# Four residual layers on one core: expert blocks beside the gates of the other half, two context chains, top-2 by VectorE's max search

## The chip, the cores and the metric

The kernel runs on one core of a Trainium2 chip. The metric is device time in microseconds (us) of one execution; less is better. The core's engines are PE (TensorE: matmuls and transposes), DVE (VectorE), ACT (ScalarE), POOL (GpSimd) and SP (here only a queue that issues DMAs; it is written SPq in the views). Each engine takes its instructions strictly in the order in which the program gives them; they meet through semaphores.

## The reference

x has 32 batches of 128 tokens of 128 values. Eight residual steps follow each other, each scaled by the tanh of a gate g. Cut to what matters:

```python
x = x + tanh(g0) * attention(heads=16, q=x_normed, kv=context)                    # "A0"
x = x + tanh(f0) * ffn(layernorm(x))                                              # "F0", hidden 512
x = x + tanh(g1) * attention(heads=16, over context and self)(layernorm(x))       # "A1"
x = x + tanh(f1) * block1(layernorm(x))     # "F1": causal attention, then 8 experts, top 2:
    t = rmsnorm(u, g2); probs = softmax(t @ router_w); vals, idx = top_k(probs, 2)
    w = vals / sum(vals); y = sum_k w_k * w2[e_k] @ (silu(w1[e_k] @ t) * (w3[e_k] @ t))    # hidden 256
x = x + tanh(g2) * attention(heads=8, kv=context)(layernorm(x))                   # "A2"
x = x + tanh(f2) * block2(layernorm(x))     # "E2": layernorm again, 8 experts, top 2, hidden 512, gelu
    tp, ti = top_k(softmax(xf @ Wg.T + bg), 2); tp = tp / (sum(tp) + 1e-8)
x = x + tanh(g3) * depool(layernorm(x), ctx)       # "context" work: norm of ctx, scan, picked rows
x = x + tanh(f3) * bitlinear_ffn(layernorm(x))     # quantized, hidden 512
```

## The kernel before

A planner written in Python (`make_plan`) decides the order of all work before the kernel is built. Each `do(kind, ...)` appends one step; each engine's program then walks through the list of steps and issues its part of each. So the order of the `do` calls is the order on every engine's queue and on SP's DMA queue. `reckon` gives the planner a cost in ns for each step by engine, and the planner keeps a clock for each engine from them. Work that is not part of the main loop is put on a list `side` with `soon` or `chain` (a chain is a list of units; each goes on the list when the one before it has been issued and its tokens are due). `run_side` takes the first unit of the list, by rank (0 first) and then age, for which `can` says yes: its needs are due by the planner's clock, and the engine that it begins on is at most 3000 ns ahead of PE by that clock. `drain(done)` issues side units until `done()` holds. `now()` gives the last tokens of every engine, which a step can wait for before it reuses memory.

The main loops are the attentions (A0, A1, the causal one of F1, and A2), batch by batch, with 16 preparations of pairs of batches (norm, transpose, `split` into three bf16 parts, store to DRAM, load back) as side chains. The maxima of each batch (`max_rows`) go through three small DMAs.

The expert layers work on groups g of four batches ("fronts", `sorted_front`), 8 of them, 4 in each half h. A front of E2 is: `n0` and `n1` layernorm of X into U, `n2` the second norm into a front buffer, `n3` `gate_turn` (four transposes), `n4` `gate_logits`, `n5` `gate_exp`, `n6` `gate_rank`, `n7` `gate_pick`, `n8` `place` (a prefix sum on PE that gives each token its row in its expert's region), `n9` four times `scatter` (2 indirect DMAs by POOL each, so 8 in a front), and `x_base`. A front of F1's experts ("E1") has one norm less. Fronts of even and of odd g are two lines; g can be ranked only when g-1 is placed. When the four fronts of a half are scattered, the half is sorted, and its 24 expert blocks of 256 rows can run (`blocks`: `block_table`, then for each block load, turn, weights, up, down, store). Then `fetch` (2 indirect DMAs by POOL for a batch) and `combine` bring the results back to X.

The stages around the change, in the order of the plan:

- F1's attention, with the fronts of E1 beside it; when half 0 is sorted, its blocks run beside the rest of the attention. Then `drain(lambda: not side)`: all fronts and all blocks of half 0 are finished. `after_f1 = now()` stands behind that drain.
- half 1's blocks of E1 beside the first 9 steps of A2 (at step 9 the plan drains until they are stored), then `moe2_load`, then the rest of A2 with fetches and combines of E1, with fronts of E2 as side work.
- `drain(lambda: not side)` again: all fronts of E2 are finished. Then one chain with half 0's blocks of E2, `half(0)` (fetches, and the last two layers' own work `own(g)` for g 0 to 3, in 2 lanes), half 1's blocks, `half(1)` (g 4 to 7, in 4 lanes). Beside it one chain of `setup` and the eight contexts `context(g)`: `cx_load`, `ends`, `end_marks`, a norm, `picks`, `up_scale`, `depool`, `pick_rows`. `own(g)` can pass `x4` (`x3_add`) only when the context of g is there.

On SP's queue `q_load` (the last layer's weights) waits for its need and holds everything behind it; DVE waits in its own `q_load` too.

Of the kernel before, what the change touches and what calls it, by code (L numbers as in the profile page):

```python
# [9 lines left out]
I32 = mybir.dt.int32  # L10
F32R = mybir.dt.float32r
# [85 lines left out]
def reckon(s):  # L97
# [218 lines left out]
class Memory:  # L316
    def __init__(self, nc, ctx, io):
# [58 lines left out]
        self.LG = sb("LG", [128, 2, 4, 8])  # L376
        self.GT = sb("GT", [128, 2, 4, 8])
# [60 lines left out]
        self.GM, self.DD = CF[:, 3840:4352], CF[:, 5376:5888]  # L438
        self.UP, self.CX = VSF[:, 0:512], VAF[:, 0:1024].rearrange("p (b d) -> p b d", b=4)
# [11 lines left out]
        self.EB = self.r32[:, :, :].rearrange("p a b -> p (a b)").bitcast(BF16)[:, 0:512].rearrange("p (k t) -> p k t", k=4)  # L451
# [45 lines left out]
def make_plan():  # L497
# [706 lines left out]
    E1 = experts_of(0, gi=5, chunks=2, xf=(("HB", 6), ("HB", 7)), t=(0, 1), big="big_at0", weight="router_w", scale="g2", bcol=None, plus=None)  # L1204
    E2 = experts_of(1, gi=6, chunks=4, xf=(("AT", 0), ("sp32", 0)), t=(2, 3), big="big_at", weight="WgT", scale="gamma", bcol="beta", plus=1e-8)

    def sorted_front(E, g):
        got, b0, k, h = {}, 4 * g, g % 2, g // 4

        def n0():  # L1210
            got["s"] = norm_in(("X", b0), 4, xs(b0, 4), twice="second")

        def n1():
            if E.i:
                got["u"] = norm_out(got["s"], ("U", b0), None, done="u")
                for j in range(4):
                    u_done[b0 + j] = got["u"]
            else:
                got["s"] = norm_in(("U", b0), 4, us(b0, 4), rms=True)

        def n2():
            got["n"] = norm_out(got["s"], E.xf[k], (E.xf_free[k], E.begin), second=(("U", b0), got["u"]) if E.i else None)
# [49 lines left out]
        return [*([n0] if E.i else []), n1, n2, n3, n4, n5, n6, n7, n8, *[(lambda j=j: n9(j), lambda: got["p"]) for j in range(4)], (base, ())]  # L1272

    def blocks(E, h, t_w, start, bank):
# [5 lines left out]
        def table():  # L1280
# [1701 lines left out]
```

## Time and profile before

| | |
|---|---|
| time, median of 3 runs (lowest to highest) | 2334.78 us (2333.24 to 2337.86) |
| the profiled execution, own time | 2332.09 us |
| its span, first to last instruction | 2330.3 us |
| busy: PE, PE weight loads | 1703.6 us (73%), 1207.5 us (52%) |
| busy: DVE, ACT, POOL | 1318.2 us (57%), 1025.1 us (44%), 684.4 us (29%) |
| mean granted TensorE clock | 0.832 of full speed |

The views used below: a table of stretches gives busy time of each engine in each stretch of the span, with granted clock (PEclk) and DMA share. A timeline gives instructions in order of time, merged when the same one follows itself (x4), with the idle time before them and what released them in brackets. Groups by line give count, busy us, mean ns of one, and idle time before. Times of a timeline are us from the start of the span.

### The profile page before, as it was taken

Reading aid. Unit: us, or ns where it says so; the run is one execution under the profiler, and the core shown is the slowest. Engines: PE = TensorE matmul, PEld = TensorE weight load, DVE = VectorE, ACT = ScalarE, POOL = GpSimd, SP = SyncE. Lnnn points to the kernel's source line nnn. Section 1 sums busy time; section 2 is a strip of 40 time slices with the busy share of each in tenths; the row PEclk is TensorE's granted clock in tenths of the full one; section 3 lists DMA queues with packets and bytes.
Section 4 is the critical chain, followed back from the end, with each engine's and each line's share of the span. In section 5 each row is a group of like instructions: output and inputs, shape, how many; then the busy total and the mean of one; then the engine's idle time right before and its main releaser. Section 6 shows DMA issues by size and latency. Waiting matters only on the chain. (4 is left out here: it accounts for less than half of the span.)

```text
span 2330.3 us, 42245 instructions
## 1 busy us (share of the span) xinstructions
PE 1703.6 (73%) x14898; PEld 1207.5 (52%) x14902; DVE 1318.2 (57%) x3879; ACT 1025.1 (44%) x2073; POOL 684.4 (29%) x1123
## 2 busy tenths in 40 slices
PE   2758879999679888899879974675473298687144
PEld 1435547677467666655545663554242187566032
DVE  4656664533456676557766543553577722365475
ACT  2435543433256565544434443442242065477165
POOL 4322100100422222134442124323535600612430
PEclk9978889999878888889988997886576599799566
DMA  6545546300155455312222122444360222212100
GB/s 176 125 85 113 124 145 201 73 1 0 25 101 96 90 111 97 92 45 54 52 54 59 43 64 59 102 121 144 84 138 28 66 62 71 77 51 64 36 19 19
DMA packets 189757, 184.47 MB, mean 79 GB/s; under 512 B 29508, under 2 KB 177924, under 8 KB 183556
## 3 DMA queue, kind: packets, MB, share of 16 engines
q1 hardware_dynamic: 180540, 145.04, 26.9%
q10 hardware_dynamic: 816, 19.92, 2.9%
q0 software_dynamic: 8192, 16.79, 2.5%
q8 instruction: 122, 2.00, 0.4%
q14 instruction: 87, 0.71, 0.1%
HBM read 119.47 MB, written 80.74 MB: 86 GB/s over the span
## 5 line engine op out<-in xcount | busy, mean ns | idle before, releaser
L2100 DVE TENSOR_REDUCE mneg<-psb 128x4 f32<-128x512 f32 (+1 forms) x576 | 386.1, 684 | 245.2 <-PE psb L1711 197.5
L2505 ACT ACTIVATE HB<-psb 128x512 f32<-128x512 f32 x384 | 222.8, 597 | 208.5 <-PE psb L1711 194.1
L1711 PE MATMUL psb<-K,Q 96*128 96x128 bf16 x1280 | 188.1, 249 | 68.1 <-DVE mneg L2100 37.7
L2738 POOL TENSOR_SCALAR rs<-mv 128x2 f32<-128x2 f32 (+1 forms) x96 | 22.7, 237 | 702.0 <-DVE mv L2060 693.0
L2505 ACT ACTIVATE HB<-psb,bias 128x512 f32<-128x512 f32 x192 | 132.0, 687 | 209.5 <-PE psb L1711 170.0
L1711 PE MATMUL psb<-Q,K 99*128 99x128 bf16 x1280 | 144.6, 244 | 92.2 <-DMA Q<-mT 91.0
L1711 PEld LDWEIGHTS psb<-K,Q 96*128 96x128 bf16 x1280 | 112.0, 111 | 125.5 <-DVE mneg L2100 50.8
L1711 PEld LDWEIGHTS psb<-Q,K 99*128 99x128 bf16 x1280 | 106.8, 111 | 125.4 <-issue 110.5
L1711 PE MATMUL psb<-K 128*128 128x256 f32 x576 | 152.4, 412 | 2.9 <-issue 2.1
L1711 PE MATMUL psb<-KS,Q 96*128 96x128 bf16 x1024 | 150.6, 238 | 4.8 <-DVE mneg L2100 4.3
L1711 PE MATMUL psb<-HB,VA 128*9 128x128 f32 (+1 forms) x2560 | 147.8, 307 | 8.1 <-ACT OE L2510 4.5
L1711 PEld LDWEIGHTS psb<-K 128*128 128x128 f32 x576 | 113.2, 207 | 18.9 <-issue 3.9
L1711 PE MATMUL psb<-HB,VS 128*9 128x128 f32 (+1 forms) x2048 | 109.7, 289 | 11.6 <-ACT OE L2510 7.5
L1711 PE MATMUL psb<-Q,KS 99*128 99x128 bf16 x1024 | 108.5, 233 | 2.2 <-DMA Q<-mT 2.2
L1711 PE MATMUL psb<-cnegb,identb 128*128 128x512 bf16 x256 | 107.4, 420 | 0.5 <-issue 0.5
L2318 DVE TENSOR_TENSOR K<-psb,HB 128x256 f32<-128x256 f32 x48 | 20.4, 424 | 153.2 <-PE psb L1711 114.1
L1723 PE MATMUL psb<-cst,OE 128*128 128x128 f32 x480 | 95.4, 324 | 14.6 <-ACT OE L2510 11.0
L1711 PEld LDWEIGHTS psb<-KS,Q 96*128 96x128 bf16 x1024 | 91.4, 106 | 25.8 <-issue 11.2
L1711 PEld LDWEIGHTS psb<-WB,HB 128*128 128x128 f32 x768 | 96.2, 197 | 14.8 <-issue 12.2
L1711 PE MATMUL psb<-WB,HB 128*128 x768 | 96.4, 280 | 9.9 <-ACT HB L2590 9.9
L1711 PE MATMUL psb<-biasT,selbb 96*128 96x512 bf16 x192 | 91.1, 474 | 1.8 <-issue 1.8
L1711 PEld LDWEIGHTS psb<-Q,KS 99*128 99x128 bf16 x1024 | 79.5, 105 | 22.2 <-issue 10.6
(464 smaller groups left out, 3984.0 us busy)
## 6 DMA issues: line engine op xcount, KB each, us to landing
tok_rows<-in_zero ACTq DMA_DIRECT2D x16, 1152.0 KB, 31.6
K<-sc_k SPq DMA_DIRECT2D x32, 384.0 KB, 5.2
Q<-sc_q SPq DMA_DIRECT2D x32, 384.0 KB
sc_q<-comp SPq DMA_DIRECT2D x48, 192.0 KB
K<-tok_rows SPq DMA_DIRECT2D x72, 128.0 KB
y_rows<-K SPq DMA_DIRECT2D x72, 128.0 KB
sc_q<-comp SPq DMA_DIRECT2D x48, 128.0 KB
vraw<-in_ctx SPq DMA_DIRECT2D x48, 128.0 KB, 6.8
```

Of the source, the lines that this page charges most:

```text
L1711: return pe.e.matmul(out, w, x, start=start, stop=stop, skip_group_check=True)
L1723: t = pe.e.transpose(o[:, 128 * j:128 * j + 128], src[:, 128 * j:128 * j + 128], ident)
L2100: t = e.tensor_reduce(m.mneg[:, s.b % 4, s.i * A.per:(s.i + 1) * A.per], PSB[s.use.bank].rearrange("p (h k) -> p h k", h=A.per), AX.X, ALU ...
L2318: v.done(e.tensor_tensor(y2, o2, m.b2bc[:, bass.ds(at_, 128)].unsqueeze(1).broadcast_to([128, 2, 128]), ALU.add), s.use.drained)
L2505: a.done(act(m.HB[:, s.slot, :], PSB[s.use.bank], ACT.Exp, bias=bz), s.use.drained)
L2738: then(e.tensor_scalar(r0, var, EPS, None, ALU.add))
```

## The change

Eight edits, in the planner unless said otherwise:

1. `after_f1` is taken right after the last step of F1's attention, and the drain behind it ends when half 0's blocks of E1 are done and half 1 is sorted, instead of when nothing is left. Half 1's blocks start as soon as half 1 is sorted and the attention is planned (`second1`). The two halves' block loads and stores get separate semaphores.
2. The drain behind A2 is gone. The blocks of E2 begin when half 0 is sorted (`table` returns False until then, and is tried again later).
3. The last layer's `setup` and the contexts begin when E2's half 1 is sorted (`third`), and the contexts run as two chains (even and odd g) with two sets of buffers (GM, DD, UP, CX, EB).
4. `gate_logits` finds the 8 values in order with `e.max` and their places with `e.max_index`, 4 of each; `gate_rank` and its 256-wide comparisons are gone; the softmax's sum is no longer needed but for E2's 1e-8.
5. `gate_pick` computes the two weights from two exponentials and the masks from the found indices.
6. `norm_out` of all fronts (two in E2, one in E1) goes from DVE to ACT. For E2's first norm POOL then adds a product and a negation (`shift`).
7. `x_base` stands ahead of the four scatters instead of behind them.
8. Ranks: E1's fetches 2 instead of 1; half 1's fetches of E2 2 instead of 1. Planner costs of the gate steps: see the diff.

```diff
-        "gate_logits": lambda: (("pe", 300), ("dve", 650)),
+        "gate_logits": lambda: (("pe", 1900), ("dve", 2200)),
         "gate_exp": lambda: (("act", 250),),
-        "gate_rank": lambda: (("dve", 2600),),
-        "gate_pick": lambda: (("dve", 2800),),
+        "gate_pick": lambda: (("dve", 1600),),
...
+        self.GM, self.DD = [CF[:, 3840:4352], CF[:, 4864:5376]], [CF[:, 5376:5888], CF[:, 4352:4864]]
+        self.UP = [VSF[:, 0:512], VSF[:, 512:1024]]
+        self.CX = [a.rearrange("p (b d) -> p b d", b=4) for a in (VAF[:, 0:1024], self.xn[:, :, :].rearrange("p a b -> p (a b)"))]
...
-            got["s"] = norm_in(("X", b0), 4, xs(b0, 4), twice="second")
+            got["s"] = norm_in(("X", b0), 4, xs(b0, 4), twice="second", by="act")
...
-                got["u"] = norm_out(got["s"], ("U", b0), None, done="u")
+                got["u"] = norm_out(got["s"], ("U", b0), None, done="u", by="act")
...
+            got["n"] = norm_out(got["s"], E.xf[k], (E.xf_free[k], E.begin), second=(("U", b0), got["u"]) if E.i else None, by="act")
...
-            do("gate_rank", g=g, big=E.big, need=got["t"], free=E.begin, done=inc("dve", "ranked"))
-
-        def n7():
             got["k"] = inc("dve", "picked")
-            do("gate_pick", g=g, i=E.i, big=E.big, plus=E.plus, gi=E.gi, need=t_tg, done=got["k"])
+            do("gate_pick", g=g, i=E.i, plus=E.plus, gi=E.gi, need=(got["t"], t_tg), done=got["k"])
...
-        return [*([n0] if E.i else []), n1, n2, n3, n4, n5, n6, n7, n8, *[(lambda j=j: n9(j), lambda: got["p"]) for j in range(4)], (base, ())]
+        return [*([n0] if E.i else []), n1, n2, n3, n4, n5, n6, n8, (base, ()), *[(lambda j=j: n9(j), lambda: got["p"]) for j in range(4)]]
...
+            if E.sorted[h] is None:
+                return False
...
+    after = {}
+
+    def second1():
+
+        if "f1" not in after:
+            return False
+        chain(blocks(E1, 1, t_m, after["f1"], misc), 3)
+        return None
+
     def end1(h):
-        if h == 0:
-            chain(blocks(E1, 0, t_m, E1.begin, misc), 3)
+        chain([second1] if h else blocks(E1, 0, t_m, E1.begin, misc), 3)
...
     run_f1()
-    drain(lambda: not side)
-    after_f1 = now()
+    after_f1 = after["f1"] = now()
+    drain(lambda: E1.done[0] and E1.sorted[1])
...
-    E2.begin, E2.end = after_f1, lambda h: None
+    E2.begin, E2.end = after_f1, lambda h: third() if h else None
...
-    chain(blocks(E1, 1, t_m, after_f1, misc), 3)
     begin2()
-    chain([(lambda b=b: fetch1(b), lambda b=b: E1.stored[b // 16] or ()) for b in range(B)], 1)
+    chain([(lambda b=b: fetch1(b), lambda b=b: E1.stored[b // 16] or ()) for b in range(B)], 2)
...
     run2(more)
-    drain(lambda: not side)
...
+    def third():
+
+        L3["units"] = setup, context, *_ = layer3((now(), E2.xf_free))
+
+        def contexts():
+            for c in range(2):
+                chain([f for g in range(c, NG, 2) for f in context(g)], 1)
+
+        chain([*setup, contexts], 1)
...
     def half(h):
+        if "units" not in L3:
+            return False
...
-        chain([(lambda b=b: fetch2(b), ()) for b in range(16 * h, 16 * h + 16)], 1)
+        chain([(lambda b=b: fetch2(b), ()) for b in range(16 * h, 16 * h + 16)], 1 + h)
...
-    chain([*setup, *[f for g in range(NG) for f in context(g)]], 1)
...
-        v.wait_ge(v.step(e.tensor_reduce(s0, L, AX.X, ALU.max)))
-        v.done(e.tensor_tensor(L, L, wide(s0), ALU.subtract), s.done)
-
-    def gate_rank(s):
-        _, L, T, s0, s1 = gate_views(s.g)
-        big0, big1 = big(s.big)
-        v.wait_ge(s.need, s.free)
-        v.wait_ge(v.step(e.tensor_reduce(s0, L, AX.X, ALU.add)))
+        for j in range(4):
+            t = e.max(V[:, j, :], L[:, j, :])
+        v.wait_ge(v.step(t))
+        v.done(e.tensor_tensor(E, m.LG[:, s.g % 2], V[:, :, 0:1].broadcast_to([128, 4, 16]), ALU.subtract), s.done)
+        for j in range(4):
+            t = e.max_index(ix[:, j, :], V[:, j, :], L[:, j, :])
+        v.step(t)
+
+    def gate_pick(s):
+        bs = slice(4 * s.g, 4 * s.g + 4)
+        E, ix, s0, s1 = m.EG[:, s.g % 2], m.ix[:, s.g % 2], m.small[:, 0, bs], m.small[:, 1, bs]
+        M, ek = m.pick, m.ek[:, s.i, :, bs]
+        v.wait_ge((v.chain, v.n), s.need)
+        t = v.step(e.tensor_copy(ek.rearrange("p k b -> p b k"), ix[:, :, 0:2]))
+        t2 = v.step(e.tensor_tensor(s0, E[:, :, 8], E[:, :, 9], ALU.add))
+        v.wait_ge(t)
+        number = C("blocks")[:, 0:8].unsqueeze(1).unsqueeze(1).broadcast_to([128, 2, 4, 8])
+        v.wait_ge(v.step(e.tensor_tensor(M[:, :, :, :], number, ek.unsqueeze(3).broadcast_to([128, 2, 4, 8]), ALU.is_equal)))
+        v.done(e.tensor_tensor(m.pickb[:, :, :], M[:, 0], M[:, 1], ALU.add), s.done)
+        if s.plus:
+            v.wait_ge(v.step(e.tensor_reduce(s1, E[:, :, 0:8], AX.X, ALU.add)))
+            v.wait_ge(v.step(e.scalar_tensor_tensor(out=s0, in0=s1, scalar=s.plus, in1=s0, op0=ALU.mult, op1=ALU.add)))
         v.wait_ge(v.step(e.reciprocal(s1, s0)))
-        v.wait_ge(v.step(e.tensor_tensor(L, L, wide(s1), ALU.mult)))
-        pj = L.unsqueeze(2).broadcast_to([128, 4, 8, 8])
-        pi = L.unsqueeze(3).broadcast_to([128, 4, 8, 8])
-        low = C("low").rearrange("p (i j) -> p i j", i=8).unsqueeze(1).broadcast_to([128, 4, 8, 8])
-        e.tensor_tensor(big0, pj, pi, ALU.is_gt)
-        v.wait_ge(v.step(e.tensor_tensor(big1, pj, pi, ALU.is_equal)))
-        v.wait_ge(v.step(e.tensor_tensor(big1, big1, low, ALU.mult)))
-        v.done(e.tensor_tensor(big0, big0, big1, ALU.add), s.done)
-        v.wait_ge(s.done)
-
-    def gate_pick(s):
-        bs, L, T, s0, s1 = gate_views(s.g)
-        big0, _ = big(s.big)
-        M = m.pick
-        v.wait_ge(v.step(e.tensor_reduce(T, big0, AX.X, ALU.add)))
-        e.tensor_scalar(M[:, 0], T, 0.5, None, ALU.is_lt)
-        e.tensor_scalar(M[:, 1], T, 1.0, None, ALU.is_equal)
-        e.tensor_scalar(m.pickb[:, :, :], T, 1.5, None, ALU.is_lt)
-        v.wait_ge(v.step(e.scalar_tensor_tensor(out=T, in0=T, scalar=1.5, in1=L, op0=ALU.is_lt, op1=ALU.mult)))
-        v.wait_ge(v.step(e.tensor_reduce(s0, T, AX.X, ALU.add)))
-        if s.plus:
-            v.wait_ge(v.step(e.tensor_scalar(s0, s0, s.plus, None, ALU.add)))
-        v.wait_ge(v.step(e.reciprocal(s1, s0)))
-        v.wait_ge(s.need)
-        v.wait_ge(v.done(e.scalar_tensor_tensor(out=T, in0=T, scalar=tg[:, s.gi:s.gi + 1], in1=wide(s1), op0=ALU.mult, op1=ALU.mult), s.done))
-        pk = m.prod[:, :, :, :]
-        v.wait_ge(v.step(e.tensor_tensor(pk, M[:, :, :, :], T.unsqueeze(1).broadcast_to([128, 2, 4, 8]), ALU.mult)))
-        v.wait_ge(v.step(e.tensor_reduce(m.gk[:, s.i, :, bs], pk, AX.X, ALU.add)))
-        number = C("blocks")[:, 0:8].unsqueeze(1).unsqueeze(1).broadcast_to([128, 2, 4, 8])
-        v.wait_ge(v.step(e.tensor_tensor(pk, M[:, :, :, :], number, ALU.mult)))
-        v.wait_ge(v.step(e.tensor_reduce(m.ek[:, s.i, :, bs], pk, AX.X, ALU.add)))
+        v.step(e.scalar_tensor_tensor(out=m.gk[:, s.i, :, bs].rearrange("p k b -> p b k"), in0=E[:, :, 8:10], scalar=tg[:, s.gi:s.gi + 1],
+                                      in1=s1.unsqueeze(2).broadcast_to([128, 4, 2]), op0=ALU.mult, op1=ALU.mult))
...
+        if s.twice == "second" and s.by == "act":
+            then(e.tensor_tensor(r0, r0, power, ALU.pow))
+            shift()
```

## Rows read from the trace of the kernel before

**Rows 1.** Page: span, and busy us of each engine.
```profile
span 2330.3 us, 42245 instructions
PE 1703.6 (73%) x14898; PEld 1207.5 (52%) x14902; DVE 1318.2 (57%) x3879; ACT 1025.1 (44%) x2073; POOL 684.4 (29%) x1123
```
**Rows 2.** Table of stretches: PE, PEld, DVE, ACT, POOL busy us; PEclk, DMA share, GB/s.
```profile
1395.00:1420.00 25.00, 16.39 (x91) 14.19 (x89) 12.14 (x28) 12.28 (x19) 4.77 (x3) 0.84 0.16 53
...
1612.00:1750.00 138.00, 83.45 (x788) 49.34 (x788) 86.02 (x300) 47.74 (x108) 71.17 (x114) 0.66 0.52 129
...
1767.00:1859.00 92.00, 17.22 (x108) 14.25 (x108) 64.28 (x285) 5.06 (x10) 68.48 (x84) 0.50 0.16 54
1859.00:1971.00 112.00, 98.91 (x629) 88.85 (x630) 27.35 (x81) 69.28 (x151) 5.90 (x11) 0.93 0.23 70
...
2013.00:2151.00 138.00, 114.82 (x765) 99.30 (x766) 72.99 (x236) 94.44 (x211) 35.50 (x72) 0.92 0.19 58
2186.00:2330.00 144.00, 57.60 (x330) 35.43 (x332) 101.80 (x300) 71.61 (x139) 32.34 (x67) 0.59 0.06 18
```
**Rows 3.** Timeline of POOL: A2's last split; first scatters of g 1 and g 3.
```profile
1724.50 0.67 POOL L2773 TENSOR_TENSOR comp<-r,comp 128x256 bf16<-128x256 f32 x1
1767.31 1.12 POOL L2709 DMA_INDIRECT tok_rows<-sp,pidx  x1 [42.15 <-DVE pidx L2248]
...
1795.28 1.10 POOL L2709 DMA_INDIRECT tok_rows<-sp,pidx  x1 [0.54 <-issue]
```
**Rows 4.** Timeline of DVE: a gate's first and last step.
```profile
1803.01 0.18 DVE L2201 TENSOR_REDUCE small<-LG 128x4 f32<-128x32 f32 x1 [0.30 <-issue]
...
1808.02 0.22 DVE L2233 TENSOR_REDUCE ek<-prod 128x8 f32<-128x64 f32 x1
```
**Rows 5.** Groups by line, DVE, 1570 to 1862: moved norms, small steps.
```profile
L2077 DVE TENSOR_SCALAR U<-X,mv,rs 128x128 f32<-128x128 f32 x32 | 10.7, 395 | 4.8 <-POOL rs L2752 4.8
...
L2073 DVE TENSOR_SCALAR sp<-U,rs 128x128 f32<-128x128 f32 x16 | 3.5, 302 | 0.4
...
L2248 DVE CAST pidx<-pos 128x8 int32<-128x8 f32 x8 | 1.4, 171 | 0.3
```
**Rows 6.** Groups by line, ACT: a norm, the gate's exponential, a table load.
```profile
L2484 ACT ACTIVATE xn<-X,mv,rs 128x128 f32<-128x128 f32 x16 | 7.8, 585 | 2.2 <-POOL mv L2730 2.2
...
L2560 ACT ACTIVATE LG<-LG 128x32 f32<-128x32 f32 x8 | 1.8, 226 | 13.2 <-issue 7.9 <-DVE LG L2195 5.3
...
L2590 ACT ACT_TABLE_LOAD x1 | 1.3, 1283 | 0.5 <-PE psb L1711 0.5
```
**Rows 7.** Timeline of SP's queue in A2: the parts' stores, a period apart.
```profile
1709.56 1.50 SPq L2783 DMA_DIRECT2D sc_q<-comp  x3
...
1718.60 1.51 SPq L2783 DMA_DIRECT2D sc_q<-comp  x3
```
**Rows 8.** Timeline of POOL, DVE and SP: last scatter, table and first loads, E1's half 1.
```profile
1394.92 0.96 POOL L2709 DMA_INDIRECT tok_rows<-HB,pidx  x1 [0.30 <-issue]
...
1414.18 0.17 DVE L2262 TENSOR_TENSOR KS<-next,cst 128x8 f32<-128x8 f32 x1 [1.85 <-ACT K L2597]
...
1421.81 5.58 SPq L2783 DMA_DIRECT2D KS<-tok_rows  x4
```
**Rows 9.** Timeline of DVE: the last two contexts, and the end.
```profile
2213.72 0.87 DVE L2371 TENSOR_SCALAR r<-cst,bidx 128x128 bf16<-128x128 f32 x4
...
2271.01 0.87 DVE L2371 TENSOR_SCALAR r<-cst,bidx 128x128 bf16<-128x128 f32 x4
...
2298.82 0.69 DVE L2389 TENSOR_TENSOR U<-psb,rows 128x512 f32<-128x512 f32 x1 [1.29 <-PE psb L1710]
2299.71 0.69 DVE L2394 TENSOR_TENSOR U<-psb,U 128x512 f32<-128x512 f32 x1 [0.20 <-PE psb L1710]
...
2327.19 0.35 DVE L2445 SCALAR_TENSOR_TENSOR X<-psb,sc,X 128x128 f32<-128x128 f32 x1 [0.50 <-PE psb L1710]
```
**Rows 10.** Table of stretches, columns as in rows 2: the last 30 us.
```profile
2300.00:2330.00 30.00, 7.96 (x43) 4.39 (x44) 13.78 (x39) 12.11 (x22) 1.72 (x4) 0.60 0.03 10
```

More of the change, by code:

```diff
@@ L1218, in n1 @@
             else:
-                got["s"] = norm_in(("U", b0), 4, us(b0, 4), rms=True)
+                got["s"] = norm_in(("U", b0), 4, us(b0, 4), rms=True, by="act")
         def n2():
-            got["n"] = norm_out(got["s"], E.xf[k], (E.xf_free[k], E.begin), second=(("U", b0), got["u"]) if E.i else None)
+            got["n"] = norm_out(got["s"], E.xf[k], (E.xf_free[k], E.begin), second=(("U", b0), got["u"]) if E.i else None, by="act")
         def n3():
@@ L1438, in make_plan @@
     t_2["b2"] = dma("dma_b2")
-    L3 = {}
     def layer3(w):
-        free = {n: w for n in ("cx", "up", "dd", "gm", "eb")}
+        free = {(n, c): w for n in ("cx", "up", "dd", "gm", "eb") for c in range(2)}
         tok = {}
@@ L1621, in layer3 @@
         return setup, context, own, lane
-    setup, context, own, lane = layer3(after_a2)
+    L3 = {}
+    def third():
[4 more added lines that the diff above has]
+        chain([*setup, contexts], 1)
     ring[1] = misc_turn[1] = 8
@@ L1641, in half @@
     def half(h):
+        if "units" not in L3:
+            return False
+        _, _, own, lane = L3["units"]
         if h:
@@ L1933, in depool @@
         pe.wait_ge(s.need, s.use.before)
-        pe.done(matmul(PSB[s.use.bank], C("toep"), m.UP, True, True), s.use.full)
+        pe.done(matmul(PSB[s.use.bank], C("toep"), m.UP[s.c], True, True), s.use.full)
     def pick_rows(s):
@@ L2379, in picks @@
         v.wait_ge(s.use.full, s.free)
-        v.wait_ge(v.done(e.tensor_scalar(m.GM, PSB[s.use.bank], -1.0, 0.0, ALU.add, ALU.max), s.use.drained))
-        v.done(e.tensor_scalar(m.GM, m.GM, 127.0, C("iota_p"), ALU.min, ALU.is_equal), s.done)
+        v.wait_ge(v.done(e.tensor_scalar(m.GM[s.c], PSB[s.use.bank], -1.0, 0.0, ALU.add, ALU.max), s.use.drained))
+        v.done(e.tensor_scalar(m.GM[s.c], m.GM[s.c], 127.0, C("iota_p"), ALU.min, ALU.is_equal), s.done)
     def up_scale(s):
         v.wait_ge(s.need)
-        v.done(e.tensor_tensor(b4(m.UP), b4(m.UP), m.rows[:, 1, :].unsqueeze(1).broadcast_to([128, 4, 128]), ALU.mult), s.done)
+        v.done(e.tensor_tensor(b4(m.UP[s.c]), b4(m.UP[s.c]), m.rows[:, 1, :].unsqueeze(1).broadcast_to([128, 4, 128]), ALU.mult), s.done)
     def pick_rows(s):
@@ L2557, in gate_exp @@
     def gate_exp(s):
-        L = m.LG[:, s.g % 2]
+        E = m.EG[:, s.g % 2]
         a.wait_ge(s.need)
-        a.done(act(L, L, ACT.Exp), s.done)
+        a.done(act(E, E, ACT.Exp), s.done)
     def table(s, kind, most):
@@ L2612, in depool @@
         a.wait_ge(s.use.full, s.free)
-        a.done(act(m.DD, PSB[s.use.bank], ACT.Copy), s.use.drained)
+        a.done(act(m.DD[s.c], PSB[s.use.bank], ACT.Copy), s.use.drained)
     def x3_turn(s):
@@ L2750, in norm_in @@
         then(e.tensor_scalar(r0, r0, EPS, None, ALU.add))
-        if s.twice == "second":
+        if s.twice == "second" and s.by == "act":
+            then(e.tensor_tensor(r0, r0, power, ALU.pow))
+            shift()
+        elif s.twice == "second":
             done(e.tensor_tensor(r0, r0, power, ALU.pow), s.rstd)
@@ L2887, in cx_load @@
         sp.wait_ge(s.free)
[L2888 removed]
+        load(f"cx{s.c}", m.CX[s.c], io["ctx_2048"][4 * s.g:4 * s.g + 4].rearrange("b t d -> t b d"))
     def out_store(s):
```

79 lines of the change are left out of this document (36 added, 43 removed).

## The prediction

> **What bounds the kernel now.** I read the page first: PE is busiest with 73%, DVE 57%, so no engine bounds the whole span [rows 1]. Averages over eight stages say little, so I took the table of stretches next, at the places that the change touches [rows 2]. The reader is to see four different limits there. From 1767 to 1859 PE is busy 17.22 of 92 us at the low clock (0.50, which is 1.2 GHz), ACT 5.06, while DVE has 64.28 and POOL 68.48: A2 has ended and only fronts of E2 run, behind the drain. From 1859 to 1971 PE has 98.91 of 112: half 0's 24 blocks, PE-bound at 4.7 us each. From 2013 to 2151 PE has 114.82 of 138 (half 1's blocks beside own work). From 2186 to the end DVE has 101.80 of 144, PE 57.60.
>
> Then the timeline of POOL in the first of these: the scatters of g 1 begin at 1767.31 and those of g 3 at 1795.28, two fronts later, so a front takes 14.0 us of POOL (8 scatters and the norm), and before the first of them POOL had waited 42.15 us for `pidx` [rows 3]. Only g 0 was placed before A2 ended; the other seven fronts form the 92 us. On SP's queue A2's stores are 9.04 us apart for a pair of batches [rows 7]. At the end, DVE starts the last two contexts only at 2213.72 and 2271.01; the last one's rows come at 2298.82, `x3_add` of g 7 follows at 2299.71, and 28 us for that one group alone close the kernel [rows 9]. Of the last 30 us DVE works 13.78 and ACT 12.11: latency, not throughput [rows 10].
>
> **The change part by part.** Everything is set against the profiled execution's own 2332.1 us; its span is 2330.3 [rows 1], and the median of the runs is 2.7 above.
>
> *Start of E1's half 1.* Its last scatter begins at 1394.92 and takes 0.96; allowing 3 us to land it is sorted at 1399. Its table begins at 1414.18, behind half 0's last block operation, and its first loads at 1421.81 [rows 8]. The edit may use 15 us of this, but half 0's last blocks keep PE busy 16.39 of 25 us there [rows 2], and both halves share three PSUM banks. Take 12 of 15, bounds 0 and 25 (the upper with the 8 us of table and load gap hidden too). The last front of E1 itself is shorter: 2, bounds 0 and 8.
>
> *The gates.* From the sum to the expert numbers a gate takes DVE 1803.01 to 1808.24, 5.2 us [rows 4], and 0.6 ahead of it. New: about eight small steps in pick, 0.2 each as their like, 1.6; two in logits, 0.4; and 4 `max` and 4 `max_index`, which this trace doesn't show. Nearest is a 128x8 step at 0.171 [rows 5]: eight of them 1.4, bounds 0.8 (overlapped) and 2.8 (double). Value 1.5, as they have the same 8 elements. So 3.5 instead of 5.8: 2.3 saved, 37 for 16 gates. The norms take 4 x 0.395 and 4 x 0.302 = 2.8 from DVE in each E2 front [rows 5], and put 4 x (0.59 + about 0.4) = 4 on ACT [rows 6]; one norm in E1, about 1.1. Altogether DVE loses 37 + 22 + 9 = 68 us. Most of it is off the path: in the fronts' own stretch POOL's 14.0 sets the pace, and the `shift` makes it 0.5 longer. What it does change is the order: the planner refuses units that begin on DVE while DVE's clock is ahead, and a front now begins fewer of them there and books 3.8 instead of 6.05 us of DVE for a gate. POOL's 42 us of waiting inside A2 can take three fronts.
>
> *No drain behind A2.* Half 0 of E2 needs g 3 scattered. Fronts 1 and 2 had their statistics in A2 already; with lighter gates I expect 1 and 2 scattered inside A2 and g 3 at its end. Then comes `block_table` with 6 us and a load: blocks start 15 us behind A2's end instead of 92. Gain 77; bounds 84 (table and load only, 8) and 43 (g 1 to 3 all behind A2, 3 x 14.0, and the table).
> What this costs: A2 gets the fronts' DVE work, some 7 us each, for three of them 21, against 138 - 86.02 = 52 idle [rows 2]; +6, bounds 0 and 30. The other four fronts now run beside PE-bound blocks: their PE work is 17.22 for six to seven, so 2.6 each at the low clock, 10 for four at most; the in-order queue adds waits on `pidx`, and the high clock of the blocks (0.93) takes some off. +10, bounds 3 and 25. `q_load` waits on SP for g 7's scatters, and every block load and store is queued behind it, and on DVE the additions of `block_down`: once, +5, bounds 0 and 15.
>
> *Table loads.* gate_exp now falls among gelus. The trace shows one load when the first gelu comes, 1.283 us [rows 6], none between exponentials and tanhs. Four fronts make up to eight more, 10 us of ACT; it has 112 - 69.28 = 43 idle [rows 2], so I add nothing beyond the +10 above.
> The Trainium skill (ScalarE: Activation LUTs, sections on what ACT_TABLE_LOAD costs and on table sets) speaks against this mixing: exp and tanh share a set, gelu has its own, and each switch costs the load of about 1283 ns and a drain of about 1380. The trace agrees on the load. By the page eight switches would be an estimated 21 us instead of 10, and if none were hidden the time would be 21 later.
>
> *Contexts.* Two of eight leave the tail. Beside the blocks they meet PE with 23 idle in half 1's stretch [rows 2]: +4, bounds 0 and 10. In the tail DVE loses two contexts: `ends` 0.87, the last row step 0.69 [rows 9], and some six steps of that kind between, an estimated 5 each, 10 in all. More important, g 7 no longer waits, so that its 28 us stand beside the other groups instead of behind them: of the last 30 us DVE's 16 idle [rows 10] can go but for the ends of a chain. I take 15 of the 16, so 25 with the contexts; bounds 5 (half a context's DVE time, the idle only moved) and 40 (most of the tail's 42 idle us gone [rows 2]).
>
> *At nothing:* `x_base` earlier, the ranks of the fetches, the separate semaphores; they add no instruction. The fetches' POOL bursts stay.
>
> **Sum:** 2332.1 - 12 - 2 - 77 + 6 + 10 + 5 + 4 - 25 = 2241, with the median's habit of lying a little above, 2242.
>
> **The rivals.**
> *The fronts stay late* (g 1 to 3 behind A2): for it speaks that the planner's combines and attention still outrank them, against it POOL's 42 idle us. 28 us more: 2270.
> *Everything overlaps*: with DVE 68 us lighter, A2 isn't stretched (-6), blocks aren't slowed (-10), q_load costs nothing (-5), blocks start 8 behind A2 (-7), F1 gains 8: 2206.
> *The tail keeps its length*, since four groups' latency chains and POOL's norms, not the context, set it: 25 more, 2267.
> *The overlap doesn't come about*: the planner still places the blocks behind the fronts; only E1 and the tail gain a little, 2315.
> *Slower:* POOL's order. A pair of A2 visits POOL twice (norm, split). If a front's scatters (8 x 1.27 = 10.2 us) stand ahead of both, a pair takes up to 20 instead of 9.04 us [rows 7]; over the 11 pairs of A2's second part +120, which beats the gains of 91 and gives 2361. It decides from 91 / 11 = 8.3 us a pair. Against it: the last split is at 1724.50, 42 us before g 1's scatters [rows 3], so preparations run ahead.
>
> **How the numbers follow.** Forecast 0.45 (its own range 2215 to 2265), everything overlaps 0.22, fronts late 0.17, tail unchanged 0.06, no overlap 0.03, slower 0.05, and 0.02 for a sum of mishaps that ends level. The range leaves out the last three and the edges: 2185 (the better case and 21 below) to 2298. Faster by over 0.2% (about what this measurement can tell from no change) 0.93, same 0.02, slower 0.05.
>
> **What would show it.** In the profile after: scatters of g 1 to 3 before A2's last batch; no stretch with PE under 3 tenths between A2 and the blocks; exponentials and up to eight table loads among the gelus; half 1's first loads of E1 before half 0's last stores; `ends` eight times before the last block; the end less than 120 us behind the last block's store. Wrong would make it: POOL saturated inside A2 with longer SP periods, SP's queue standing at q_load, or blocks far slower than 4.7 us.

## The result, and the profile after

The changed kernel takes 2267.2 us (median of 4 runs, 2262.3 to 2270.7) where the kernel before takes 2334.0 in the same comparison: ratio 0.971, 95% interval 0.968 to 0.974. Forecast were 2242 in a range of 2185 to 2298, and faster with 0.93. The direction and the range held; of the 91 us forecast, 67 came. The profiled execution took 2270.65 us.

The page of the changed kernel, span and busy time by engine:
```profile
span 2268.5 us, 42224 instructions
PE 1694.8 (75%) x14899; PEld 1196.8 (53%) x14902; DVE 1252.3 (55%) x3759; ACT 1054.9 (47%) x2175; POOL 684.7 (30%) x1139
```
Against [rows 1] DVE lost 65.9 us (68 were forecast) and ACT gained 29.8. Where the time of the span went is read from the places where stages meet. Timelines of the changed kernel, DVE, POOL and SP: E1's half 1 loads; g 2's placement and first scatter; the second attention's last addition; g 3's placement, first and last scatter; half 0's table, and its first load.
```profile
1411.79 1.44 SPq L2781 DMA_DIRECT2D KS<-tok_rows  x2
...
1756.02 0.17 DVE L2243 CAST pidx<-pos 128x8 int32<-128x8 f32 x1
...
1758.31 1.10 POOL L2704 DMA_INDIRECT tok_rows<-AT,pidx  x1 [0.47 <-issue]
...
1759.78 0.35 DVE L2150 SCALAR_TENSOR_TENSOR X<-otmp,tg,X 128x128 f32<-128x128 f32 x1
...
1771.00 0.17 DVE L2243 CAST pidx<-pos 128x8 int32<-128x8 f32 x1
...
1772.77 1.10 POOL L2704 DMA_INDIRECT tok_rows<-sp,pidx  x1 [0.46 <-issue]
...
1781.74 0.96 POOL L2704 DMA_INDIRECT tok_rows<-sp,pidx  x1 [0.30 <-issue]
...
1784.06 0.17 DVE L2257 TENSOR_TENSOR HB<-next,cst 128x8 f32<-128x8 f32 x1 [12.23 <-DMA tok_rows<-sp,pidx]
...
1790.76 1.49 SPq L2781 DMA_DIRECT2D K<-tok_rows  x2
```
The blocks start at 1790.76 where they started at 1859.25: 68.5 us earlier, 31 us behind the attention where it was 92. But g 3's scatters end 23 us behind the attention, not at its end, and g 2's begin only 1.5 us before it.

Tables of stretches, cut to the microsecond at the stores of half 0's last block, half 1's first and half 1's last: first the kernel before, then the changed one (PE, PEld, DVE, ACT, POOL busy us; PEclk, DMA share, GB/s).
```profile
1859.00:1978.00 119.00, 104.39 (x672) 93.95 (x672) 30.74 (x94) 72.24 (x159) 7.57 (x15) 0.93 0.22 68
1978.00:2013.00 35.00, 14.95 (x59) 10.88 (x59) 11.45 (x44) 7.66 (x16) 21.17 (x22) 0.70 0.26 76
2013.00:2151.00 138.00, 114.82 (x765) 99.30 (x766) 72.99 (x236) 94.44 (x211) 35.50 (x72) 0.92 0.19 58
2151.00:2330.00 179.00, 61.83 (x346) 37.03 (x348) 108.07 (x322) 82.65 (x162) 58.06 (x95) 0.60 0.10 28
```
```profile
1791.00:1927.00 136.00, 111.00 (x696) 99.40 (x696) 36.93 (x185) 85.11 (x182) 41.83 (x56) 0.89 0.21 69
1927.00:1977.00 50.00, 15.25 (x61) 12.09 (x61) 18.62 (x85) 7.61 (x16) 36.62 (x47) 0.66 0.26 76
1977.00:2125.00 148.00, 122.29 (x835) 105.73 (x834) 88.20 (x281) 102.83 (x236) 27.43 (x67) 0.93 0.20 64
2125.00:2268.00 143.00, 55.79 (x320) 32.09 (x322) 98.11 (x284) 76.61 (x151) 54.95 (x87) 0.60 0.09 27
```
The reader is to see that from the first block load on, the two kernels take nearly the same: 471 us before, 478 after. Half 0 is 18 us longer, the gap between the halves 14, half 1 11, and the tail 36 shorter. The whole gain of the span, 61.8 us, is the earlier start, 68.5, less 6.7.

A timeline merges stores that follow each other and gives the start of the first. So the last store of half 1 is found by itself only in a narrow window; first the kernel before, then the changed one:
```profile
2151.35 0.32 SPq L2783 DMA_DIRECT2D y_rows<-K  x1
```
```profile
2125.49 0.32 SPq L2781 DMA_DIRECT2D y_rows<-K  x1
```

### The profile page after: what moved, and what is told of

It reads as the page before. It is cut to its first block and busy times, and to the rows that moved or that the text cites. A ratio compares the mean times of both kernels' runs of the same rounds, so it can differ in the third digit from the quotient of the medians.

```text
span 2268.5 us, 42224 instructions
## 1 busy us (share of the span) xinstructions
PE 1694.8 (75%) x14899; PEld 1196.8 (53%) x14902; DVE 1252.3 (55%) x3759; ACT 1054.9 (47%) x2175; POOL 684.7 (30%) x1139
## 5 line engine op out<-in xcount | busy, mean ns | idle before, releaser
L2733 POOL TENSOR_SCALAR rs<-mv 128x2 f32<-128x2 f32 (+1 forms) x96 | 21.8, 227 | 702.5 <-DVE mv L2081 694.4
L1732 PE MATMUL psb<-K,Q 96*128 96x128 bf16 x1280 | 183.3, 245 | 64.8 <-DVE mneg L2121 39.8
L1732 PE MATMUL psb<-K 128*128 128x256 f32 x576 | 161.4, 428 | 24.0 <-ACT K L2566 7.3
L1732 PE MATMUL psb<-KS,Q 96*128 96x128 bf16 x1024 | 145.7, 232 | 6.0 <-DVE mneg L2121 6.0
L1732 PEld LDWEIGHTS psb<-K 128*128 128x128 f32 x576 | 118.2, 217 | 43.8 <-issue 14.7
L1732 PE MATMUL psb<-WB,HB 128*128 x768 | 102.6, 289 | 12.7 <-ACT HB L2585 10.0
L1732 PEld LDWEIGHTS psb<-WB,HB 128*128 128x128 f32 x768 | 101.3, 205 | 18.8 <-issue 15.9
L1744 PE MATMUL psb<-cst,OE 128*128 128x128 f32 x480 | 95.9, 326 | 17.0 <-ACT OE L2505 13.5
L2585 ACT ACTIVATE HB<-psb,cols 128x256 f32<-128x256 f32 x192 | 76.7, 475 | 34.0 <-PE psb L1732 14.3
```

The costliest lines, as they stand in the source:

```text
L1732: return pe.e.matmul(out, w, x, start=start, stop=stop, skip_group_check=True)
L1744: t = pe.e.transpose(o[:, 128 * j:128 * j + 128], src[:, 128 * j:128 * j + 128], ident)
L2585: t = act(h[:, 256 * (o + c):256 * (o + c) + 256], PSB[u.bank][:, 256 * c:256 * c + 256], ACT.Gelu, bias=m.cols[:, bass.ds(at_ + (m.col_at ...
L2733: then(e.tensor_scalar(r0, var, EPS, None, ALU.add))
```

## The experiments

Stages of each profiled execution, in us, worked out from its timelines, each store by itself (end of the second attention A2; from there to the first block load; half 0 to its last store; to half 1's first store; to its last; tail), and the ratio to the kernel before in the same runs. Runs with one letter ran on one chip; a, b and c differ from d and e in a way that the last section tells, so a variant is compared with the changed kernel of its kind.

| run | A2 ends | to load | half 0 | gap | half 1 | tail | load to end | ratio |
|---|---|---|---|---|---|---|---|---|
| before (a) | 1767 | 92 | 118 | 36 | 138 | 179 | 471 | 1 |
| changed (a) | 1760 | 31 | 137 | 49 | 149 | 143 | 478 | 0.971 |
| e11 changed (b) | 1764 | 31 | 135 | 49 | 145 | 143 | 472 | 0.972 |
| e9 (b) | 1789 | 31 | 132 | 49 | 145 | 143 | 469 | 0.974 |
| e10 (b) | 1759 | 45 | 132 | 50 | 144 | 142 | 469 | 0.970 |
| e12 (c) | 1761 | 31 | 156 | 35 | 131 | 156 | 478 | 0.972 |
| e5 changed (d) | 1684 | 33 | 123 | 29 | 159 | 138 | 449 | 0.956 |
| e6 (d) | 1714 | 83 | 122 | 21 | 143 | 180 | 465 | 0.997 |
| e7 (d) | 1668 | 43 | 115 | 29 | 159 | 139 | 442 | 0.950 |
| e8 (d) | 1683 | 32 | 125 | 26 | 171 | 141 | 464 | 0.965 |
| e1 (e) | 1693 | 88 | 125 | 25 | 136 | 138 | 425 | 0.971 |
| e2 (e) | 1681 | 32 | 122 | 29 | 96 | 254 | 502 | 0.980 |
| e3 (e) | 1687 | 32 | 129 | 26 | 148 | 157 | 460 | 0.959 |
| e4 (e) | 1695 | 33 | 121 | 29 | 163 | 139 | 451 | 0.957 |

e1 to e5 have the same program up to A2's end, and it still scatters from 1681 to 1695 among them, so of the single profiles only the later columns are read closely. Some expectations below take the start of merged stores for the last one: their gaps of 59, 45, 38 and 31 us (changed kernel, before, e4, e3) are 49, 36, 29 and 26 store by store, and their 171 us tail of e3 is 157.

**e1: the drain back.**
```diff
+    drain(lambda: E2.sorted[1])
     ring[1] = misc_turn[1] = 8
```


> The changed kernel with one thing put back: behind the second attention the planner again runs nothing but the experts' fronts until the last scatter of half 1 is planned, and only then half 0's expert blocks; gates, norms and context chains stay new. In the changed kernel the first block load comes 31 us behind the attention's end, and half 0's blocks take 135 us where they took 112 alone. Theory (the overlap is worth its start, less what the fronts cost the blocks that they run beside): with the drain the load comes some 75 to 85 us behind the attention, +50, and the blocks run alone, -20: about 2267 + 30 = 2297 us. Rival (the slower blocks have another cause than the fronts, and stay slow): +50 whole, 2317 us. Rival (the new gates alone make the drain short, the overlap is worth nothing): 2267 to 2272 us.

Measured: 2203.2 us, ratio 0.971 (0.969 to 0.974). The changed kernel has 0.956 (0.952 to 0.960) beside a kernel before of the same time (2266 against 2268), so the drain costs 37 us (two chips of one kind), near the 30 of the theory. But its parts came otherwise: the load comes 54 us later, and what is won back is 24 us over the whole stretch to the end, none of it in half 0 (125 us against 123) and 23 of it in half 1. The contexts moved too: in e1 six of the eight begin beside half 0 and the last two as half 1's first block is stored, where e5 has two in the gap and six beside half 1.

**e2: contexts behind the blocks.**
```diff
-                chain([f for g in range(c, NG, 2) for f in context(g)], 1)
+                chain([f for g in range(c, NG, 2) for f in context(g)], 3)
```


> The changed kernel with the two context chains ranked behind the blocks (rank 3 in place of 1), so that the planner issues a context's step only where nothing else is due. Theory (the pair of contexts stands in the in-order queues in front of half 1's first block): the gap between the halves' stores falls from 59 us towards the 45 of the kernel before and half 1's blocks from 148 towards 138 us, 10 to 20 us off the last block store; if the contexts then come behind the blocks, up to 25 us are lost in the tail: 2250 to 2275 us, and the trace shows the two parts apart. Rival (the gathers of half 0 and not the contexts make the gap): last block store unchanged, 2267 us, or 2290 us with the later contexts.

With this order the output is another than the reference's (at which step wasn't looked for), so this is no usable kernel. Ratio 0.980: 53 us worse. The first pair still stood in the gap, half 1 fell to 96 us, and the tail rose to 254: the other six contexts begin only there, and `own(g)` can't pass `x4` without its context. The price was in the tail, 116 us where up to 25 were expected.

**e3 and e8: the table when due, and contexts at the blocks' rank.**
```diff
-            if E.sorted[h] is None:
+            if E.sorted[h] is None or P.late(E.sorted[h]) > 100:
                 return False
```


> The changed kernel with one condition more in the planner's table step: it isn't issued before half 0's last scatter is due to have landed (in the changed kernel VectorE stands 12.2 us in block_table's wait, with group 4's finished logits queued behind it). The table itself comes no earlier; the fronts of half 1 do. Theory (the fronts beside the blocks stand in their way): group 4's placement comes some 10 us earlier and the later fronts with it, less of them beside the blocks: 3 to 10 us, 2257 to 2264 us. Rival (nothing waits for the fronts of half 1): 2267 us, the placements earlier and the block stores where they were.

> The changed kernel with e3's condition (the block table isn't issued before the last scatter is due) and the context chains at the blocks' own rank, 2, in place of 1. Theory (what stands in front of the blocks in the in-order queues sets their pace): as e3, which had 31 us between the halves' stores and 171 us behind the last of them, and 5 to 10 us better where contexts no longer go first: ratio 0.955 to 0.959. Rival (contexts that come later make the tail longer by as much): ratio 0.959 to 0.965.

e8 has e3's edit and e2's with rank 2. Measured: 0.959 (0.957 to 0.962) and 0.965 (0.960 to 0.970), 9 and 14 us slower than the changed kernel, so neither gained; both theories fell, and e8's rival came. (e3 is set against e5 across two chips and the intervals of the ratios overlap, so its 9 us are loose.) In e3 g 5 was placed 40 us behind A2 where e5 has it at 69, but g 4 only 2 us earlier than there and g 6 17 us later. The first two contexts began 2 us before half 0's last store instead of in the gap: gap and half 1 shrank by 14 us, half 0 grew by 6 and the tail by 19. In e8 half 1 alone grew, by 12.

**e4: no exponential beside the blocks.**
```diff
-        a.done(act(E, E, ACT.Exp), s.done)
+        a.done(act(E, E, ACT.Copy if s.plain else ACT.Exp), s.done)
```


> The changed kernel with the exponential of groups 4 to 7 of the second experts left out (ScalarE copies in its place, same operands, so the weights of these groups are others): no table is loaded between the blocks' gelu and the gates. In the changed kernel 7 loads of 1.28 us lie in half 0's blocks. Theory (ScalarE does not set the blocks' pace, TensorE waits for queued fronts and weights): 0 to 4 us less, 2263 to 2267 us. Rival (each switch stalls the blocks by its load and a drain): 7 x 1.28 = 9 us to 19 us, 2248 to 2258 us.

The weights of these groups are others, the work is the same but for the loads. Ratio 0.957 (0.955 to 0.959), the changed kernel's 0.956 (0.952 to 0.960) on another chip of that kind, and 451 us from load to end against 449: no gain, and the rival's 9 to 19 us lie outside what the intervals leave (8 us). The changed kernel's timeline of ACT fits:
```profile
1814.52 0.88 ACT L2479 ACTIVATE U<-X,mv,rs 128x128 f32<-128x128 f32 x2
1815.41 1.28 ACT L2555 ACT_TABLE_LOAD   x1
1816.71 0.26 ACT L2555 ACTIVATE EG<-EG 128x64 f32<-128x64 f32 x1
```
The load starts as the norm ends and the exponential as the load ends; no further time lies beside the 1.28 us, and ACT is idle for 51 of half 0's 136 us.

**e5 and e11: the changed kernel again.** Nothing edited.

> The changed kernel itself once more, beside a kernel before that took 2268 us in the runs e1 to e4 (2334 us where the change was first timed). Nothing is edited. If the 3% lie in the attention stages alone (e1's second attention ends 67 us earlier) and are worth the same to both kernels: ratio 0.971. If the wide gap between the changed kernel's halves (59 us from store to store, 38 us in e4 with the same order of steps) belonged to that first run only: 20 us less, ratio 0.957 to 0.963, and then e3 and e4 (0.959, 0.957) have gained next to nothing against the changed kernel.

> The changed kernel, not edited, to set e9 and e10 against in the same runs. In the first comparison (ratio 0.971, kernel before 2334 us) its trace held 29 idle times of ScalarE over 2.5 us, 172 us in sum, that no semaphore and no other engine ends, 56 us of them in the 200 us of the second experts' first half; the trace of the kernel before held 24, 180 us; e5 (ratio 0.956, kernel before 2266 us) held two, 14 us. Theory (those idle times are what makes the first comparison slower, and they cost the changed kernel more because they fall on its path): if the kernel before takes 2260 to 2275 us here, ratio 0.953 to 0.960 and two such idle times; if it takes 2325 to 2340 us, ratio 0.968 to 0.974 and over 20 of them. Rival (the two ratios are scatter from run to run): a ratio that does not go with the time of the kernel before.

e5: 2166.2 us beside 2265.8, ratio 0.956 (0.952 to 0.960); the gap between the halves was 29 us. e11: 2273.5 us beside 2343.1, ratio 0.972 (0.966 to 0.977), with 30 such idle times of ACT, 168 us, and again a gap of 49. With the first comparison (0.971 beside 2334) that makes three, and the ratio goes with the time of the kernel before; the intervals rule out scatter from run to run. That the idle times of ACT are the cause is not shown by this.

**e6: the gates alone, in the kernel before.** The diff is that of the gates (`gate_logits`, `gate_pick`, their buffers and costs), nothing else.

> The kernel before with one part of the change: gates by MAX8 and FIND_INDEX8 in place of the 8 x 8 comparisons, with their costs in the planner; drains, norms and the one context chain stay as before. Theory (a third of the gain is the shorter gate, since behind the attention the placements come one gate, one norm and one turn apart, 15 us): placements 1.5 to 2.5 us closer, five of them behind the attention, 8 to 12 us there and 2 to 4 us behind the first experts' fronts: ratio 0.993 to 0.995, 12 to 16 us less. Rival (the drain is set by norms and scatters, the gate runs beside them): ratio 0.998 to 1.000.

Ratio 0.9967 (0.9946 to 0.9989): 9 us less than the kernel before, between the theory's 12 to 16 and the rival's 0 to 5. Behind the attention the placements are 13.4 to 14.2 us apart (1733.22, 1747.43, 1760.88, 1774.69, 1788.13), where they were 13.5 to 15.1, not 1.5 to 2.5 closer: POOL's 14.0 of [rows 3] sets them, and in e6 too its scatters and norms follow each other with at most 0.8 us between. The new steps, from the changed kernel's groups by line:
```profile
L2209 DVE FIND_INDEX8 ix<-LG 128x8 uint32<-128x8 f32 x64 | 9.1, 160 | 0.0
L2205 DVE MAX8 LG<-LG 128x8 f32<-128x8 f32 x64 | 6.0, 156 | 0.5
```
They overlap: four MAX8 of 156 ns take 0.37 us from 1765.07 on, and the eight steps take (9.1 + 6.0) / 16 = 0.94 us a gate, near the lower bound of 0.8, not 1.5.

**e7 and e10: the norms' engine.**
```diff
-            got["s"] = norm_in(("X", b0), 4, xs(b0, 4), twice="second", by="act")
+            got["s"] = norm_in(("X", b0), 4, xs(b0, 4), twice="second")
```
and so for the fronts' other norms; in e10 `by` is "act" for groups 3 to 7 of E2 and "dve" else.

> The changed kernel with the fronts' norms left to VectorE as in the kernel before (bias and scale by VectorE, 4 x 0.3 us and more a norm); all else stays changed. Theory (the fronts are held by each other's order and not by one engine, and VectorE is the engine with free time beside the blocks): ratio that of the changed kernel within 0.2%, 5 us either way. Rival (ScalarE was the right place: VectorE's queue delays gates and combines): 8 to 15 us slower than the changed kernel. Other rival (ScalarE's queue was what stretched half 0's blocks from 112 to 127 us): 5 to 12 us faster.

> The changed kernel with the fronts' norms by VectorE for the first experts and for groups 0 to 2 of the second (all of them beside attention), and by ScalarE from group 3 on (behind the attention and beside the blocks). In e7, with all of them by VectorE, the attention ended 16 us earlier, but the first block load came 43 us behind it where e5 had 33; the blocks took 109 us (e5 113). Theory (ScalarE is short of time beside attention, VectorE's in-order queue is what the fronts behind it wait for): the attention's gain kept, the load 33 to 36 us behind it: 4 to 8 us below e7, ratio 0.946 to 0.948. Rival (the load came later in e7 only because the attention ended earlier than group 3's front, whose place does not move): as e7, ratio 0.949 to 0.951. Other rival (blocks need ScalarE too): 3 to 5 us above e7, ratio 0.952.

e7: 2150.5 us, ratio 0.950 (0.946 to 0.954) against 0.956: 16 us faster than the changed kernel, and the fastest version found on such a chip. Its profile is 13 us shorter: A2 ends 16 earlier (the scatter of that point is nearly as large), the load comes 10 later behind A2, and 7 are won behind it, all in half 0 (115 us against 123), where the second rival had looked for them. That ACT is short beside the attention's exponentials is a reading of this, not shown by itself. The intervals of the ratios touch, the times of the runs (2150.0 to 2154.9, and 2160.0 to 2169.4) don't. e10: 0.970 (0.967 to 0.974) against e11's 0.972: no difference, on a chip of the other kind and with five of E2's eight norms left to ACT; e7's own edit wasn't run there. The theory that the load would follow A2 by 33 us fell (45). The rival that group 3's front keeps its place fell too: g 3 was placed at 1783.63, in e11 at 1775.32, though A2 ended 5 us earlier. What delays it stays open.

**e9: the first experts' wait back.**
```diff
     run_f1()
+    drain(lambda: E1.done[0] and E1.sorted[1])
     after_f1 = after["f1"] = now()
-    drain(lambda: E1.done[0] and E1.sorted[1])
```


> The changed kernel with the first experts' wait put back: the planner finishes half 0's blocks and half 1's fronts before the stage behind the feed-forward is taken as ended, so that half 1's blocks and the second attention's first steps are issued later. In the profile first taken of the changed kernel this part gave 10 us at half 1's first load and 12 us at the load of the second experts' weights. Theory (the 10 to 12 us pass whole to the end, since the attention behind them is bound by its own steps): 8 to 14 us slower than the changed kernel, ratio 0.960 to 0.963 where e5 had 0.956. Rival (the attention takes the time back, waiting for the gathers of half 1): within 3 us, ratio 0.955 to 0.958.

2284.6 us against e11's 2273.5: 11 us slower, as the theory said; the load of the second experts' weights comes at 1624.25 against 1601.21. The ratios' intervals (0.970 to 0.978, 0.966 to 0.977) overlap and the two profiled executions are 23 us apart, so the size is loose.

**e12: contexts beside half 0.** `third` is called at half 0's last scatter as well and starts setup and contexts there; `UP` moves to the attention's transpose buffer; the lanes' buffers are freed by a second call.

> The changed kernel with the third layer's setup and the two context chains begun as soon as half 0's last scatter is planned behind the attention, not when half 1's is; the contexts' normalised rows go to a tile that no front uses (the transposes' buffer of the attention) and the third layer's own lanes still wait for the fronts' buffers. Four of the eight contexts are then issued beside half 0's blocks, two before half 1's table, where the changed kernel issues the first pair behind half 0's last block. In e1 (fronts drained first, contexts from half 0 on) the stretch from the first block load to the end was 425 us, in e5 449 us, with the same contexts, gates and norms. Theory (contexts are worth most beside half 0's blocks, where TensorE and VectorE have room, and cost most in the gap and in half 1, where gathers and lanes compete with them): 10 to 20 us below the changed kernel: ratio 0.947 to 0.952 where the kernel before takes some 2266 us, 0.963 to 0.967 where it takes some 2335 to 2343. Rival (contexts, fronts and blocks together overfill half 0's queues, and half 0 gets longer by what half 1 gets shorter): within 5 us of the changed kernel, ratio 0.954 to 0.958, or 0.969 to 0.974.

Ratio 0.972 (0.970 to 0.975): the changed kernel's. The table of stretches of e12:
```profile
1792.00:1948.00 156.00, 124.35 (x794) 109.89 (x794) 66.01 (x283) 94.23 (x211) 51.80 (x80) 0.86 0.24 74
1948.00:1983.00 35.00, 14.99 (x59) 10.74 (x60) 11.37 (x44) 7.89 (x17) 20.95 (x22) 0.67 0.32 90
1983.00:2114.00 131.00, 112.75 (x747) 97.11 (x748) 69.08 (x221) 92.36 (x208) 33.40 (x68) 0.91 0.17 53
2114.00:2270.00 156.00, 54.30 (x310) 30.41 (x312) 96.28 (x286) 76.55 (x149) 53.89 (x87) 0.57 0.09 25
```
Six of the eight contexts begin beside half 0. Against e11 half 0 is 22 us longer, the gap and half 1 14 shorter each, the tail 14 longer: sum 478 against 472. The rival was right on the time; but half 0 grew by more than half 1 shrank, and the tail grew too. Contexts in one chain, in the changed kernel, weren't tried: late contexts then share memory with other steps.

## Why the prediction came out as it did

- **E1's half 1, -12 and -2:** right, 12 for 14. Loads at 1411.79 against 1421.81; the second experts' weights at 1596.53 against 1608.41, 11.9 earlier. e9 puts 11 us on it in whole runs.
- **A2 stretched, +6:** right in size. A2 ends 7.2 us earlier where 12 had been won: +5. The reason given, the fronts' DVE work, isn't shown: from 1740 to 1760, near A2's end, the granted clock was 0.50 in the changed kernel and 0.85 in the kernel before, and what this costs can't be told apart.
- **No drain behind A2, -77:** the step that failed in the sum's largest term. It said that g 1 and g 2 are scattered inside A2 and g 3 at its end, so that blocks start 15 us behind. g 1 was; g 2 was placed 4 us ahead of A2's end and g 3 11 us behind it. From 1758.31 POOL has no pause above 0.5 us: g 2's eight scatters (1.26 us apart), then the norm of g 4, which is still running when g 3's rows are ready and holds them back by about 1 us, then g 3's eight scatters, to 1782.7. The landing (1.4) and 6.7 us of table follow: 31 us, within the bounds. The gain was 61. That g 4 to 7 stand behind was right. e5 has the same on another chip (g 3 placed 12 us behind, load at 33).
- **q_load, +5:** its load goes out at 1894.37, among block loads; its part in the rest can't be told apart.
- **Blocks beside fronts, +10:** mis-sized and misplaced. I priced the four fronts by their PE work, 2.6 each. e1 takes these four out of the stretch from load to end, and it is 24 us shorter, 6 each. Half 0 doesn't show it (e5 123, e6 122, e1 125): e1 has contexts there in place of fronts, and the 23 us are won in half 1, which has lost its contexts. POOL has 161 us in that stretch in e5 and 120 in e1, DVE 242 and 223. Contexts beside half 0 with the fronts left in gained nothing (e12), which speaks for the fronts as the cause; which engine charges for them isn't shown.
- **Contexts, +4, and the tail, -25:** the mechanism was right, `ends` stands eight times before the last block's store (the last at 2108.57), and both sizes were too small. The tail fell from 179 to 143, -36. Gap and half 1 rose by 13.9 and 10.6, +24.5. Together -11.5, where I had -21. I had taken the contexts' price from PE's 23 idle us in half 1. e6 and e1 show the two context chains with the drain in both and no front beside the blocks: 465 us from load to end with one chain, whose last two contexts begin in the tail (2144.95 and 2202.16), 425 with two, the last begun at 1934.77; the tail is 180 and 138. So here this part is worth some 40 us, twice what I had (in this stretch the ranks of the fetches differ too; the chips are two of one kind). e2, e3, e8 and e12 moved the contexts with fronts beside the blocks; single stages moved by up to 22 us (in e2 by 116), and the stretch from load to end was longer than the changed kernel's each time, by 6 to 53 us. That gathers, combines, lanes and contexts are one amount of work in in-order queues, of which these edits only chose the stage that shows it, is a reading of this; nothing shows it to be a limit.
- **Table loads at nothing:** right by e4. The loads are 7 beside half 0 where the kernel before has one, 1.283 us each, as in [rows 6]. The 21 us by the rule of the Trainium skill (ScalarE: Activation LUTs, what ACT_TABLE_LOAD costs) did not come; its 1283 ns agree with the trace, its drain of some 1380 ns beside each load shows in none of these rows.
- **Gates:** DVE's sum was right (-65.9 for -68, norms included), and that most of it is off the path too: 9 us in e6 for 41 us of DVE (1318.2 before, 1277.0 in e6).
- **Norms by ScalarE:** I counted them as help to DVE only. On one kind of chip they cost 16 us (e7); on the other most of them cost nothing that shows (e10, a smaller edit). ACT's part in the attention was never read for this: a missing term.
- **At nothing:** `x_base` earlier and the ranks of the fetches were not run alone, so this stays unshown.
- **Signs:** two named ahead failed. PE was busy 6.36 of the 31 us between A2 and the blocks, under 3 tenths; and the end came 143 us behind the last block's store, not under 120. Half 1's first loads of E1 before half 0's last stores (1411.79, 1433.63), the contexts before the last block, and seven table loads among the gelus came.

In sum, on the first chip: the start came 68.5 us earlier against 12 + 2 + 77 - 6 = 85, the rest +6.7 against 10 + 5 + 4 - 25 = -6. Of the miss of 29 us in the profiled execution 16.5 are the start, nearly all of it the place of g 3's front, and 13 the rest. The rest hides two larger errors of opposite sign, read on the other kind of chip: the fronts beside the blocks cost 24 us and not 10, the contexts gave some 40 and not 21. There the rest came as -16 (e6 to e5, 465 to 449) and the whole change as 100 us. So the time that was near on one chip is in part luck, and the stages are right only as to where the gain starts. The rival nearest in time was "the tail keeps its length" (2267 forecast, 2267.2 measured), and its condition did not come: the tail fell by 36 us. "Fronts late" (2270) had two more fronts to place behind A2 than there were; the likeliest case's mechanism held with one.

## What to carry to other kernels

When a drain is taken away, count first how many units of the drained chain the next stage still needs, and where the last of them stands when the stage before ends: here one front behind that end cost 16 of the 77 us forecast. Work that moves beside other work in in-order queues can cost more than its busy time on the stage's bound engine (24 us for four fronts here, priced at 10) and can show up in another stage; compare "first load to end" as one number before believing a stage, and read the boundary of a stage from single instructions, not from a merged row. And moving work to an idle engine in one stage is read in every other stage in which that edit also applies.

## What the runs showed of the hardware that was not expected

Chips differ by more than most parts of this change. The kernel before took 2334, 2343 and 2341 us on three chips (a, b, c) and 2268 and 2266 on two (e, d); the granted clock was 0.82 to 0.84 on the first kind, and 0.84 to 0.85 on the second, 1% for 3% of the time. Each chip was used for one group of runs only, so chip and session can't be told apart. The change is worth 67 and 70 us on the first kind and 100 on the second. One pair of rows shows the difference, the same two instructions of the same program on DVE; first the changed kernel's first profile:
```profile
1833.28 0.23 DVE L2227 SCALAR_TENSOR_TENSOR gk<-EG,tg,small 128x8 f32<-128x8 f32 x1
1841.47 0.42 DVE L2313 TENSOR_TENSOR K<-psb,HB 128x256 f32<-128x256 f32 x1 [7.95 <-remote]
```
and e5:
```profile
1757.80 0.23 DVE L2227 SCALAR_TENSOR_TENSOR gk<-EG,tg,small 128x8 f32<-128x8 f32 x1
1759.65 0.43 DVE L2313 TENSOR_TENSOR K<-psb,HB 128x256 f32<-128x256 f32 x1 [1.62 <-PE psb L1732]
```
Such stops, on ACT from 2.5 to 13.4 us in the changed kernel's traces and some of them perhaps waits whose releaser the trace lost, come without a releaser within the core on PE, ACT and DVE: 8, 29 and 19 idle times over 2.5 us in the first trace of the changed kernel, none, 2 and 2 in e5's. Set side by side from A2's end, the 48 `block_gate` additions of the two traces keep their distances to 0.1 us for long stretches and then jump: 6 us more in a few blocks, 11.5 at half 0's end, 32 at half 1's first block, 21.8 at half 1's end (one jump the other way). The trace of e11, from another chip of the first kind, has the first 14 of them within 0.3 us of the first trace, and all within 5.8. So most of the stops belong to places of the program and not to chance. In the us before the stop above, the first trace has a packet on each of two instruction queues (DMA queues, 1832 to 1833: kind, packets, MB, share of the 16 engines):
```profile
q8 instruction: 1, 0.02, 5.5%
q14 instruction: 1, 0.01, 5.0%
```
but e5 has such packets at the same place without a stop. Whether the fetch of instructions is what is slower on these chips stays open; no run here changes it alone. For reading it means this: half 0, gap and half 1 grew by 43 us from before to after on the first chip, and by 25 from e6 to e5 on chip d.
